# Two graph layers over an 8192 x 8192 adjacency matrix: the change of where and how a row of sums is turned, and how the sums and the last products are laid out

## What is computed

```python
def reference(x, adj, L0_gnn_u, L1_gnn_weight, L1_gnn_bias):
    def _L0_gnn_ref(x, adj, u):
        keep = (u >= 0.1).astype(x.dtype)
        return jnp.matmul(adj, x * keep / 0.9)
    def _L1_gnn_ref(x, adj, weight, bias):
        return jnp.matmul(adj, jnp.matmul(x, weight)) + bias
    x = _layernorm(x + _L0_gnn_ref(x, adj, L0_gnn_u), axis=-1)
    x = _layernorm(x + _L1_gnn_ref(x, adj, L1_gnn_weight, L1_gnn_bias), axis=-1)
    return x
```

## Time and profile before

| | |
|---|---|
| median of 3 runs | 902.91 us (902.78 to 903.06) |
| the profiled execution, its time | 902.77 us |
| the profiled execution, its span | 901.0 us |
| PE busy | 873.1 us (97%) |
| DVE busy | 529.6 us (59%) |
| ACT, POOL busy | 30.2 us, 25.3 us |
| DMA queue that loads the tiles | 358.74 MB, 96.7% of 16 engines' span |
| mean granted TensorE clock | 0.997 of full |

### The profile page before, as it was taken

The page is one execution under the profiler, slowest core; times in us unless marked ns, Lnnn a source line. Parts: engine busy times, 40 slices in busy tenths (PEclk is TensorE's granted clock), DMA queues, the critical chain, the costliest instruction groups (busy, mean ns, idle before and its releaser), DMA issues.

```text
span 901.0 us, 13601 instructions
## 1 busy us (share of the span) xinstructions
PE 873.1 (97%) x5754; PEld 406.1 (45%) x5754; DVE 529.6 (59%) x1026; ACT 30.2 (3%) x74; POOL 25.3 (3%) x24
## 2 busy tenths in 40 slices
PE   3899999999999999999999999999999999999996
PEld 3653333333343444535354554636446456456343
DVE  6356123126145656766676667768677768768655
ACT  0100000000000000000000000000000000000011
POOL 3000000000000000000000000000000000000133
PEclk9999999999999999999999999999999999999998
DMA  9999999999999999999999999989899999999952
GB/s 373 411 416 421 420 420 420 421 421 420 420 420 422 419 420 420 420 401 410 420 420 403 413 404 380 422 352 422 359 408 419 414 417 419 420 421 419 420 242 71
DMA packets 55404, 359.60 MB, mean 399 GB/s; under 512 B 6448, under 2 KB 10544, under 8 KB 12592
## 3 DMA queue, kind: packets, MB, share of 16 engines
q1 hardware_dynamic: 55344, 358.74, 96.7%
HBM read 356.61 MB, written 2.10 MB: 398 GB/s over the span
## 4 chain that ended last, share of the span: by engine, by line
PE 92%; DMA 4%; SPq 2%; issue 1%; DVE 1%; POOLq 0%; POOL 0%; ACT 0%; DVEq 0%
PE psum L996 22%; PE psum L949 21%; PE psum L964 8%; PE psum L931 8%; PE psum L958 8%; PE psum L982 6%; PE psum L917 5%; PE psum L938 4%; PE psum L1002 4%; DMA tiles<-adj_chunks 2%; DMA tiles<-adj_t 2%; PE psum L894 1%; SPq L495 1%; PE psum L1017 1%; PE psum L1032 1%
## 5 line engine op out<-in xcount | busy, mean ns | idle before, releaser
L949 PE MATMUL psum<-tiles,stat 128*64 128x512 f32 x976 | 216.8, 593 | 0.1
L996 PE MATMUL psum<-tiles,stat 128*64 128x512 f32 x944 | 211.7, 594 | 0.0
L656 DVE TENSOR_TENSOR layer<-psum,layer 128x512 f32<-128x512 f32 (+1 forms) x143 | 98.6, 689 | 182.8 <-PE psum L996 85.6
L949 PEld LDWEIGHTS psum<-tiles,stat 128*64 128x64 f32 x976 | 69.6, 137 | 128.2 <-issue 122.5
L996 PEld LDWEIGHTS psum<-tiles,stat 128*64 128x64 f32 x944 | 66.5, 137 | 123.7 <-issue 121.4
L692 DVE TENSOR_TENSOR tiles<-tiles 128x512 f32<-128x512 f32 x90 | 62.2, 691 | 53.7 <-PE psum L940 51.7
L966 PE MATMUL psum<-tiles,stat 128*64 128x256 f32 x360 | 92.7, 380 | 0.0
L933 PE MATMUL psum<-tiles,stat 128*64 128x256 f32 x360 | 92.4, 379 | 0.0
L931 PE MATMUL psum<-tiles,stat 128*64 128x256 f32 x360 | 92.4, 379 | 0.0
L931 PEld LDWEIGHTS psum<-tiles,stat 128*64 128x64 f32 x360 | 49.3, 137 | 40.9 <-issue 20.0
L680 DVE TENSOR_TENSOR tiles<-tiles 128x512 f32<-128x512 f32 x90 | 60.6, 683 | 10.0 <-DMA tiles<-adj_t 10.0
(11 more groups left out here) (100 smaller groups left out, 849.5 us busy)
## 6 DMA issues: line engine op xcount, KB each, us to landing
tiles<-adj_t SPq DMA_DIRECT2D x306, 1024.0 KB, 13.4
tiles<-adj SPq DMA_DIRECT2D x12, 1024.0 KB, 19.2
tiles<-adj_chunks SPq DMA_DIRECT2D x12, 1024.0 KB, 20.4
tiles<-xu SPq DMA_DIRECT2D x4, 1024.0 KB, 7.9
tiles<-adj_parts SPq DMA_DIRECT2D x16, 256.0 KB, 17.7
x_res<-x SPq DMA_DIRECT2D x16, 128.0 KB, 13.9
out<-layer SPq DMA_DIRECT2D x8, 256.0 KB, 2.1
w<-weight SPq DMA_DIRECT2D x4, 16.0 KB, 9.6
```

What stands on the lines that cost most here:

```text
L656: return dve.tensor_tensor(out=to, in0=addend, in1=to, op=ALU.add)
L949: last = pe.matmul(sum_f[i % 2][to, :], stat[:, j * C + c, 0:D], tile[:, c], start=begun.get("f") != i and c < 2, stop=ends and c >= 2, sk ...
L996: last = pe.matmul(bank[to, :], stat[:, j * C + c, D:2 * D], tile[:, c], start=c == 0, stop=c == C - 1)
```

## The change

1. **The sums of a row by halves of the columns.** Each chunk of a tile in a `first` or `both` job now makes two products of 256 columns with the same weights: the left half of the columns to partitions 0 to 63, the right half to partitions 64 to 127. `sum_f` then holds finished sums, 128 partitions by 256, with nothing to add across halves.
2. **The turn on DVE.** The job `turn` is gone from the list, and with it PE's four transposes and ACT's copy. At `row_end` DVE itself adds the layer's sums (two adds of 64x256), transposes `halves` in 32x32 blocks (one instruction, 128x256), adds x in eight instructions of 32 partitions by 128 elements, and goes straight on to the mean, the variance and h (`normalise`), with `sum_stat` behind. So that the 32x32 blocks put nodes where they belong, the host writes the 512 columns of every block row but the first in another order (by halves of the partitions).
3. **The pieces of chunk jobs** in the filler of later rows stand after three half-jobs and not at its start (only one such piece is left by then, in row 2's filler).
4. **The last products** take weights 64 columns wide, because a half of the partitions is what now lies side by side, and 64 moving columns: 16 products a final job in place of 8 (12 for the one that holds block row 0).

```diff
-            if pieces and (i > 1 or len(filler) % 2 == 0):
+            if pieces and (len(filler) == ECHO_BANKS if i > 1 else len(filler) % 2 == 0):
...
-                jobs.append(("turn", i - 1) if i > 1 else ("part_turn", PARTS - 1))
+                if i == 1:
+                    jobs.append(("part_turn", PARTS - 1))
...
-    jobs += again[:1]
-    jobs.append(("turn", NB - 1))
-    jobs += again[1:]
+    jobs += again
...
+        def columns_of(i, c, half):
+            return slice(c * P, (c + 1) * P) if i == 0 else slice(half * B // 2 + c * D, half * B // 2 + (c + 1) * D)
...
-                    i = job[1]
-                    act.wait_ge(turned_ready, turns(i - 1))
-                    act.wait_ge(tile_jobs_done, done_after[job])
-                    other = slice(D, P) if i >= EARLY and i % 2 == 0 else slice(0, D)
-                    act.activation(halves[other, :], sum_f[i % 2][other, :], ACT.Copy).then_inc(half_by_act, 1)
-                elif job[0] == "turn":
...
+            def turn(i):
+                k = turns(i) - 1
+                dve.wait_ge(s_res[i % 2], 16 * (i // 2 + 1))
+                dve.wait_ge(h_ready, k)
+                source = sum_f[i % 2] if i < EARLY else halves
+                last = dve.transpose(turned[:, 0:B // 2], source[:, 0:B // 2])
+                if i < EARLY:
+                    last.then_inc(half_by_dve, 1)
+                    dve.wait_ge(half_by_dve, turns(i))
+                else:
+                    step(last)
+                t = turned[:, 0:B // 2].rearrange("p (c e f) -> p c e f", c=C, f=QUAD)
+                x_rows = x_res[:, i % 2].rearrange("p (c d) -> p c d", c=C)
+                for side in range(2):
+                    for features in range(2):
+                        for e in range(2):
+                            at = slice((2 * side + features) * QUAD, (2 * side + features + 1) * QUAD)
+                            to = slice((2 * side + e) * QUAD, (2 * side + e + 1) * QUAD)
+                            f = slice(features * QUAD, (features + 1) * QUAD)
+                            last = dve.scalar_tensor_tensor(out=r[to, :, f], in0=t[at, :, e], scalar=KEPT, in1=x_rows[to, :, f],
+                                                            op0=ALU.mult, op1=ALU.add)
+                            if (side, features, e) != (1, 1, 1):
+                                last.then_inc(dve_step, 1)
+                nonlocal steps
+                steps += 7
+                dve.wait_ge(dve_step, steps)
+                last.then_inc(turned_read, 1)
+                dve.wait_ge(turned_read, k + 1)
+                normalise(i, slice(0, C))
+                if EARLY <= i < NB - 2:
+                    sum_stat(i)
+                if i == NB - 2:
+                    centre_weights()
...
-                    if i < EARLY:
-                        dve.tensor_copy(halves[D:P, :], sum_f[i % 2][D:P, :]).then_inc(half_by_dve, 1)
-                    else:
+                    if i >= EARLY:
+                        dve.wait_ge(turned_ready, PARTS)
                         dve.wait_ge(added, n_second)
-                        dve.tensor_tensor(out=halves[of_row(i), :], in0=sum_f[i % 2][of_row(i), :],
-                                          in1=layer1_pair(i)[of_row(i), :], op=ALU.add).then_inc(half_by_dve, 1)
-                elif job[0] == "turn":
-                    turn(turns(job[1]) - 1, job[1], slice(0, C))
-                    if EARLY <= job[1] < NB - 2:
-                        sum_stat(job[1])
+                        own = layer1_pair(i)[of_row(i), :]
+                        step(dve.tensor_tensor(out=halves[0:D, 0:B // 2], in0=sum_f[i % 2][0:D, 0:B // 2],
+                                               in1=own[:, 0:B // 2], op=ALU.add))
+                        dve.tensor_tensor(out=halves[D:P, 0:B // 2], in0=sum_f[i % 2][D:P, 0:B // 2],
+                                          in1=own[:, B // 2:B], op=ALU.add).then_inc(half_by_dve, 1)
+                        dve.wait_ge(half_by_dve, turns(i))
+                    turn(i)
...
                         if begun.get("f") != i:
-                            pe.wait_ge(half_by_act, turns(i - 2))
+                            if i <= 2:
+                                pe.wait_ge(half_by_act, turns(i - 2))
                             pe.wait_ge(half_by_dve, turns(i - 2))
                         ends = jobs[at + 1] == ("row_end", i)
                         for c in range(C):
-                            to = low if c % 2 == 0 else high
-                            last = pe.matmul(sum_f[i % 2][to, :], stat[:, j * C + c, 0:D], tile[:, c],
-                                             start=begun.get("f") != i and c < 2, stop=ends and c >= 2,
-                                             skip_group_check=True)
+                            for to, columns in (low, left), (high, right):
+                                last = pe.matmul(sum_f[i % 2][to, left], stat[:, j * C + c, 0:D], tile[:, c, columns],
+                                                 start=begun.get("f") != i and c == 0, stop=ends and c == C - 1,
+                                                 skip_group_check=True)
                         begun["f"] = i
...
-                elif kind == "turn":
-                    i = job[1]
-                    pe.wait_ge(turned_read, turns(i) - 1)
-                    pe.wait_ge(half_by_act, turns(i))
-                    pe.wait_ge(half_by_dve, turns(i))
-                    for c in range(C):
-                        last = pe.transpose(turned[:, c * P:(c + 1) * P], halves[:, c * P:(c + 1) * P], ident[:, :])
-                    last.then_inc(turned_ready, 1)
...
-                        for to, at in (c, slice(0, D)), (C + c, slice(D, P)):
-                            last = pe.matmul(product[n_final % 2][:, to], layer2[at, i // 2, c * P:(c + 1) * P],
-                                             w2[at, :], start=True, stop=True)
+                        for half in range(2):
+                            for row, at in (0, slice(0, D)), (1, slice(D, P)):
+                                if i + row == 0 and half:
+                                    continue
+                                to = slice(0, P) if i + row == 0 else slice(half * D, (half + 1) * D)
+                                last = pe.matmul(product[n_final % 2][to, row * C + c, 0:D],
+                                                 layer2[at, i // 2, columns_of(i + row, c, half)], w2[at, 0:D],
+                                                 start=True, stop=True)
...
-    a = np.asarray(adj).reshape(NB, P, C, NB, P, C).transpose(0, 3, 4, 5, 2, 1)
+    a = np.asarray(adj).reshape(NB, 2, P // 2, C, NB, P, C).transpose(0, 4, 5, 6, 1, 3, 2)
+    a = np.ascontiguousarray(a).reshape(NB, NB, P, C, C, P)
+    a[0] = np.asarray(adj)[:B].reshape(P, C, NB, P, C).transpose(2, 3, 4, 1, 0)
```

More of the change, by code:

```diff
@@ L34 @@
 C = 4
+QUAD = 32
 B = C * P
@@ L319, in resnorm_graph_layers @@
     for job in jobs:
-        if job[0] in ("row_end", "turn"):
+        if job[0] == "row_end":
             chain_at = done_after[job]
@@ L515, in _ @@
             pool.wait_ge(turned_read, turns(NB - 1))
-            pool.wait_ge(turned_ready, turns(NB - 1))
             pool.wait_ge(h_ready, turns(NB - 1))
@@ L729, in combine, with normalise @@
                 plus(second[:, right], t_2).then_inc(combined, 1)
-            def turn(k, i, c):
+            def normalise(i, c):
                 n = c.stop - c.start
-                t = turned[:, :].rearrange("p (c f) -> p c f", c=C)[:, c]
                 rows, squares = r[:, c, :], sq[:, c, :]
[L736 to L747, removed]
                 centre(rows, n)
@@ L752, in turn, with turn_part @@
                                          in1=over_features(rstd[:, 0, c]), op0=ALU.mult, op1=ALU.mult).then_inc(h_ready, 1)
+            def turn_part(q):
+                rows = r[:, q:q + 1, :]
+                t = turned[:, :].rearrange("p (c f) -> p c f", c=C)[:, q:q + 1]
+                dve.wait_ge(s_res[0], 16)
+                if q:
+                    dve.wait_ge(h_ready, q)
+                dve.wait_ge(turned_ready, q + 1)
+                step(dve.scalar_tensor_tensor(out=rows, in0=t[:, :, 0:D], scalar=KEPT,
+                                              in1=x_res[:, 0].rearrange("p (c d) -> p c d", c=C)[:, q:q + 1],
+                                              op0=ALU.mult, op1=ALU.add))
+                dve.scalar_tensor_tensor(out=rows, in0=t[:, :, D:2 * D], scalar=KEPT, in1=rows,
+                                         op0=ALU.mult, op1=ALU.add).then_inc(turned_read, 1)
+                dve.wait_ge(turned_read, q + 1)
+                normalise(0, slice(q, q + 1))
@@ L779, in _ @@
                 elif job[0] == "part_turn":
-                    turn(job[1], 0, slice(job[1], job[1] + 1))
+                    turn_part(job[1])
                 elif job[0] in ("chunk", "rest", "early"):
@@ L797, in _ @@
```

(15 more changed lines are left out.)

## The result

| | before | changed |
|---|---|---|
| median (lowest to highest), 4 runs each | 902.98 us (902.78 to 903.07) | 898.31 us (898.11 to 898.45) |
| ratio, 95% interval | | 0.995 (0.9938 to 0.9962) |
| span of the profiled execution | 901.0 us | 896.5 us |
| PE busy, records | 873.1 us, 5754 | 863.1 us, 6790 |
| DVE busy | 529.6 us | 560.9 us |

The forecast was 897.0 us, 5.9 less than before; the measured gain is 4.7 us. The sign, the range (893 to 902.5) and the place of the main gain hold. Three of the sum's terms and one start value don't, and they cancel in part.

The account below looks back on a forecast made before the run. Saturated DMA was taken to bound the kernel before 323 us, PE's own products and a short tail after. Span 901.0 - 7.3 + 0.6 + 0.8 = 895.1 us, giving a time of 897.0 us, range 893 to 902.5.

Parts of the forecast that it names:

- The turn on DVE: DVE's longer work at each row end was to finish the first join by T + 8.8, upper bounds T + 9.9.
- The last products: Final jobs at the end: no change for seven, 0.8 us lost on the last one, bounds 0 and 1.5.
- the sum's terms: Span of 901.0 us, less 7.3 for the turns, plus 0.6 for 256-column products, plus 0.8 for the last job.
- The turn leaves PE: Four transposes fewer on PE at each of 15 row ends, 0.67 to 0.69 us each; 7.3 us reach the end.
- That all PE instructions of these tiles double is no cost of its own: Tiles with 256-column products: records can follow at 0.055 us, only 0.108 needed, so the doubled count was to cost nothing.
- PE doesn't wait: Behind row ends: the first join ends before PE wants a fourth echo bank, 10.3 us after the row's end.
- DVE starts at T + 0.38: Start of DVE's work at a row end, 0.38 us after T, the start of row 11's filler on PE.
- the rival with the echo banks: First join later than 10.3 us after a row's end makes PE wait: 904 us or slower; chance 0.18.
- more comes through: Final jobs run on four array corners, 4 us less (893.0), or early turns count, 3 us; chance 0.15.
- The bound from the earlier trace, 0.055 us a record: Final jobs: 32 records at the closest sustained pace need 1.75 us in place of 0.9, 0.85 us above.
- the four signs that the prediction named for being wrong: PE waits for L656 after row ends; final job far from 1.1 us; tile waits after 330 us; `sum_f` products not side by side.
- The rival that it takes the gain back: Loads: if the DMA rate doesn't rise where slots free earlier, the saved 6.9 us become waits, 902; chance 0.07.

Follow-up runs that it names:

- e3: Changed kernel with four idle PE transposes per turn put back in rows 1 to 4 alone; 898.18 us.
- e10: Kernel before with nine idle PE waits ahead of each tile job, about 1900 more instructions; 903.09 us.
- e11: Kernel before with sixteen idle PE waits ahead of each of the first 150 tile jobs; 903.66 us.
- e8: Changed kernel with the piece of chunk jobs in row 2's filler back at the filler's start; 899.74 us.
- e7: Changed kernel with the eight small DVE adds of each turn made twice, same result; 919.82 us.
- e5: Changed kernel with its last products moving 128 columns again, weights still 64 wide; 901.41 us.
- e4: Changed kernel with the last final job's products sorted, 64-column weights first, then 128-column ones; 897.57 us.

## Why the prediction was right, and where it wasn't

**The turn leaves PE: right in size, right in where it counts.** 0.67 to 0.69 us a turn, ten of which were to reach the end; nine do. The ledger has 0.63 to 0.70 for rows 9 to 15. Rows 6 and 7 have 0.58 and 0.66, with nine and eight of the tiles that cost 0.012 us more between them. Row 8 has 0.06, as the margin of 2.5 us that the tiles had at 442 us in the kernel before was used up by then: they land 2.1 us later, two late landings (423 and 437 us) in. That the four turns before 287.5 us bring nothing is shown by the ledger (-0.03) and by e3.

**"That all PE instructions of these tiles double is no cost of its own": wrong, 1.5 us.** I expected PE 0.4 us ahead at 324 us; it is 1.07 us behind, because this tile lands 1.5 us later. PE's longer instruction stream is fetched in 54 packets of 16 KB in place of 46. In the kernel before, the changed kernel and e10, tiles land 1.2 to 1.6 us late behind fetch 9 and fetch 17. The seventeenth is at 363.6 us in the kernel before, behind the last point where PE waits for tiles, and at 291.8 us in the changed one, ahead of it. e11 brings it forward in the kernel before and finds the cost, e10 puts it just behind the point and finds none. Shown is that a longer stream brings the late landing forward and that it costs where the tiles set the time.

Why every eighth fetch, the traces show in part. A load reports its end in 16 parts, and the tile is there with the last of them. In the changed kernel, behind fetch 9, one part of each tile comes 1.42 us or more after the other fifteen, and it keeps this distance while the queue is full; behind fetch 10 a second part has come down to it. Fetches 11 to 16 change the last part's distance from the first by less than 0.03 us, and fetch 17 adds another 1.44 us to it. In the traces of all thirteen kernels here the last part falls back behind fetch 9 (0.8 to 1.6 us) and behind a fetch eight later, 17, by 0.8 to 1.5; only e8 has its second step at fetch 12. There the load queue had gaps (DMA share 0.76 at 203 to 206 us, 0.26 at 211 to 213), all 16 parts come within 0.3 us behind them, and the next step after 12 is at 20. So a fetch seems to hold back one of 16 parallel paths, eight of them in turn, and the ninth meets one that was behind already. The trace doesn't name the path of a fetch, so this reading fits but isn't shown.

**The turn on DVE.** The block transpose was taken at 0.45 and is 0.46. The eight adds were taken at 1.79, with an overlap seen between two unlike instructions; they take 2.52 us and 0.1 to the next, the upper bound that I had put at 2.6. The first join of row 11 ends at T + 9.7, not at 8.8, still before 10.3, so "PE doesn't wait" holds for rows 7 to 13. The step that failed is "DVE starts at T + 0.38", read in row 11 and used for all rows. In rows 14 and 15 `combine` ends later than the row does, and in row 15 two joins stand behind it too. Row 14 adds 1.08 us for the weights behind h, which the sum had left out. 1.49 and 0.38 us are lost at the two. The mechanism of the rival with the echo banks was right down to its threshold: e7 crosses it and pays 2.1 us in most rows.

**The last products: the wrong value between the right bounds, in both directions.** Seven jobs were taken unchanged, with bounds from 0.5 below to 0.85 above; each is 0.47 below, 3.2 us in all. This was the rival "more comes through" in part. The bound from the earlier trace rows, 0.055 us a record, was a pace set by 128 moving columns (e5: 0.110 us for each four) and no limit of issue. The Trainium skill's "TensorEngine Tiling (Array Packing)" (Key Properties) had it right, that four 64x64 tiles load and multiply in parallel: 0.058 us for four records of 64 columns. The Trainium skill's "TensorE: Matmul & The Clock Gate" (Back-to-back issue gap) gives about 62 ns per MATMUL where instructions aren't decoded in hardware. The records here come much faster, at 0.015 us in a job that waits for nothing and at 0.029 us right after a wait (e4); whether that case holds on this chip no run shows. For the last job, 0.8 us was taken and 1.8 is what the tail lost (the end is 1.33 us nearer to the kernel before than pair(0,15), and the final job ahead of it had gained another 0.46). About 0.4 of this is a wait: the last job can't start before the last join is done, at 886.05. Form changes cost more here than the 0.1 us read at the turn: sorting saves 0.83 us of the job in e4. (The job has twelve products, not eleven; the seven form changes are counted rightly.)

**The sum, put right:** the forecast -5.9, +1.5 for the late tile, +1.9 for rows 14 and 15, -3.2 for the final jobs, +1.0 for the last one, +0.2 for rows 6 to 14 (row 8 brings 0.6 less, the others together 0.4 more), gives -4.5 us of span, as measured. The errors against the kernel make 4.6 us and those for it 3.2, each by itself over half of the gain. That the sum came out only 1.3 us off is in good part luck. Three of the four signs that the prediction named for being wrong are in the profile: waits for L654 (L656 in the kernel before) behind rows 14 and 15, final jobs well under 1.1 us, and waits for tiles after 330 us.

**DMA.** The rate was expected at 415 to 420 GB/s between 383 and 740 us and is 403 and 407 in the two windows. The rival that it takes the gain back holds for row 8 alone: behind 326 us PE's weight loads wait for tiles twice, 0.6 us in all, and both waits are there.

## What to carry to other kernels

Where two engines are both near 97%, find the last point at which one waits for the other; what is saved ahead of it is worth nothing, and what makes a load late ahead of it is paid but for the margin that was left there. Here that was a longer instruction stream. A margin at a repeated step is to be read at the row where the engine enters it latest, not at a typical one, and everything queued behind the step belongs to it. Small products with 64 rows and 64 columns of weights ran four at a time here; they were at their fastest where they stood together by form and no wait came right before them.

## What the runs showed of the hardware

- Four records of 64x64 weights start within 0.02 us and, from the second four on, the next four follow after 0.058 us with 64 moving columns and 0.110 us with 128 (changed kernel, e5).
- Eight DVE adds of 32 partitions by 128 elements take 2.52 us, 0.315 each without any overlap, and a 32x32-block transpose of 128x256 float32 takes 0.46 us, against 0.42 for an add of 128x256 (L743 in the kernel before).
- With a full DMA queue, behind the ninth and the seventeenth fetch of PE instructions the last of a tile's 16 parts falls back by 0.8 to 1.6 us and stays there (twelve of thirteen traces; 9, 12 and 20 in e8, whose load queue had gaps in between). In the two traces of the changed kernel the tiles concerned land within 0.1 us of the same time.
- Right after a wait PE starts records of 64x64 weights every 0.029 us, where those of the job before come at 0.015 us (e4).
